# Sending rows to their expert's region of DRAM during the middle block, in a Macaron layer of MoE, Mamba-2 and MoE

## The reference

```python
x = L0_attn_x
x = x + 0.5 * _L0_ffn_ref(_layernorm(x, axis=-1), L0_ffn_router_w, L0_ffn_w1, L0_ffn_w2)
x = x + _L0_attn_ref(_layernorm(x, axis=-1), L0_attn_W_in, L0_attn_conv_w, L0_attn_conv_b, L0_attn_dt_bias, L0_attn_A_log, L0_attn_D, L0_attn_norm_weight, L0_attn_W_out)
x = x + 0.5 * _L0_ffn_ref(_layernorm(x, axis=-1), L0_ffn_router_w, L0_ffn_w1, L0_ffn_w2)
```

```python
logits = jnp.einsum('btd,ed->bte', x, router_w)
top_vals, top_idx = jax.lax.top_k(logits, K)
top_w = jax.nn.softmax(top_vals, axis=-1)
h = jnp.einsum('nd,edh->enh', xf, w1)
h = jnp.square(jax.nn.relu(h))
y = jnp.einsum('enh,ehd->end', h, w2)
```

## Time and profile before

| | us |
|---|---|
| median of three runs | 1234.97 (1228.63 to 1237.66) |
| the profiled execution, its own time | 1231.04 |
| span in its profile | 1229.3 |
| busy PE, DVE, ACT, POOL | 1000.4, 856.4, 663.3, 597.1 |
| granted PE clock, mean | 0.924 |
| first FFN, middle block, second FFN start at | 3.8, 353.1, 900.8 |

### The profile page before, as it was taken

How to read it: one execution, slowest core, us unless ns; L and a number is a source line. 1 busy time by engine, 2 the same in 40 slices (tenths; PEclk the granted TensorE clock), 3 DMA queues, 4 the chain that set the end, 5 groups by cost and what they waited for, 6 DMA issues and landing times. The chain is left out here.

```text
span 1229.3 us, 22312 instructions
## 1 busy us (share of the span) xinstructions
PE 1000.4 (81%) x6980; PEld 868.6 (71%) x7012; DVE 856.4 (70%) x1764; ACT 663.3 (54%) x1624; POOL 597.1 (49%) x608
## 2 busy tenths in 40 slices
PE   4936999999936788888988898989826999999950
PEld 4835999999824556666766666656515999999950
DVE  5586777777638778787778777775366777777647
ACT  1334777777514465656465646565313777777630
POOL 6503666667321446464545453647502466666510
PEclk9998999999966799999899989999757999999985
DMA  8404555555422111111111100000002555655449
GB/s 256 155 1 161 177 172 191 172 173 172 134 83 65 39 40 44 43 44 44 44 44 44 43 27 12 25 18 27 18 13 89 178 201 196 189 190 187 163 139 324
DMA packets 91409, 133.23 MB, mean 108 GB/s; under 512 B 11672, under 2 KB 61344, under 8 KB 91296
## 3 DMA queue, kind: packets, MB, share of 16 engines
q1 hardware_dynamic: 69024, 85.65, 20.8%
q0 software_dynamic: 13824, 37.77, 10.5%
q10 hardware_dynamic: 8448, 8.39, 2.0%
HBM read 96.12 MB, written 35.65 MB: 107 GB/s over the span
## 5 line engine op out<-in xcount | busy, mean ns | idle before, releaser
L463 POOL DMA_INDIRECT ys_d<-xs,row_of x144 | 145.3, 1009 | 158.5 <-ACT xs L551 130.5
L458 POOL DMA_INDIRECT xs<-xn_d,token_of x144 | 146.3, 1016 | 129.9 <-DVE token_of L858 86.6
L876 DVE TENSOR_TENSOR h<-h,pH 128x512 f32<-128x512 f32 (+1 forms) x80 | 50.8, 635 | 120.9 <-ACT h L533 120.6
L1684 DVE SCALAR_TENSOR_TENSOR acc<-bank,cwh,acc 128x511 f32<-128x511 f32 (+2 forms) x120 | 89.6, 747 | 40.8 <-ACT acc L1298 38.0
L871 DVE TENSOR_TENSOR w1l<-raw,w1h 128x512 fp32r<-128x512 f32 x160 | 109.7, 686 | 3.3 <-ACT w1h L528 0.5
L528 ACT ACTIVATE w1h<-raw 128x512 fp32r<-128x512 f32 x160 | 99.5, 623 | 0.6 <-DMA raw<-in_L_ffn_w_dram 0.6
L680 PE MATMUL pY<-w2h,h2h 128*128 x576 | 98.3, 292 | 1.0 <-DVE h2l L881 1.0
L1202 POOL TENSOR_TENSOR yv<-yv,sz 128x512 f32<-128x512 f32 x32 | 40.7, 1272 | 117.3 <-DVE yv L1723 114.1
L881 DVE TENSOR_TENSOR h2l<-h,h2h 128x512 fp32r<-128x512 f32 (+1 forms) x160 | 94.5, 630 | 0.3 <-ACT h2h L538 0.3
L680 PE MATMUL pY<-w2l,h2h 128*128 x576 | 91.4, 280 | 0.0
L680 PE MATMUL pY<-w2h,h2l 128*128 x576 | 91.3, 280 | 0.0
(11 more groups left out here) (269 smaller groups left out, 2953.0 us busy)
## 6 DMA issues: line engine op xcount, KB each, us to landing
raw<-in_L_ffn_w_dram SPq DMA_DIRECT2D x80, 512.0 KB, 3.9
m_yg<-ys_d SPq DMA_DIRECT2D x64, 128.0 KB, 2.2
xs<-ys_d SPq DMA_DIRECT2D x12, 512.0 KB, 6.3
wst<-in_L_ffn_w_dram ACTq DMA_DIRECT2D x8, 512.0 KB, 4.8
xs<-in_L_attn_x_dram SPq DMA_DIRECT2D x8, 512.0 KB, 5.8
xn_d<-xs SPq DMA_DIRECT2D x8, 512.0 KB, 3.9
xr<-in_L_attn_x_dram SPq DMA_DIRECT2D x32, 128.0 KB, 2.3
x_d<-xo SPq DMA_DIRECT2D x32, 128.0 KB, 2.1
```

Of the source, the lines that this page charges most:

```text
L458: pool.indirect_dma_start(out=xg[:, t % NX, :], out_offset=None, in_=xn_d, in_offset=bass.IndirectOffsetOnAxis(ap=token_of[:, t:t + 1], ax ...
L463: pool.indirect_dma_start(out=ys_d, out_offset=bass.IndirectOffsetOnAxis(ap=row_of[:, t:t + 1], axis=0), in_=y[:, t % NX, :], in_offset=No ...
L876: dve.tensor_tensor(h, h, up_bank(q, v), ALU.mult).then_inc(h2_made.sem, 1)
L1684: ins = dve.scalar_tensor_tensor(a, bank[:, 0:GT - n], cwh[:, b, HALO - n:HALO - n + 1], a, ALU.mult, ALU.add)
```

## The change

The second FFN no longer sorts. While the middle block runs, DVE picks each tile's two experts as soon as a group's scores are there (groups of `ROUTE` tiles: seven of four, one of three, one of one). PE counts, with a triangular matmul, how many earlier rows went to each expert, which gives each row its place in its expert's region of a DRAM buffer `bk_d` (8 regions of 4096 + 128 rows). POOL sends each tile there with two indirect DMAs (`send`), one for each choice. A row is 258 floats: 256 values, the row's number and its first choice. `xn2` gets 12 buffers. SP's stores to `xn_d` go.

In the second FFN the counts alone are needed: `plan_units` works out each unit's expert (`expert_i`) and first row (`row_i`). SP writes 128 zero rows behind the end of each region and a block of dead rows, waits for these nine, and then loads each unit as one plain block (`load_unit`, six buffers). The inversion, `token_of` and the gathers are gone there. Where a result goes is worked out from the two extra columns of its rows (`find_rows`). POOL's six tables at the start become others of like size and a zero block of 16 x 258 floats. The first FFN keeps its code, moved into `sort_rows` and `invert`. The middle block has one slot more.

The diff, cut to its core:

```diff
+            def load_unit(q):
+                if q == NP:
+                    sp.wait_ge(experts_known, 2)
+                n = len(tiles_of(q))
+                if q >= RU:
+                    for t in tiles_of(q - RU):
+                        sp.wait_ge(scattered[t % NX].sem, scattered[t % NX].done(t // NX))
+                at = sp.value_load(row_i[0:1, q:q + 1], min_val=0, max_val=DEAD + (E - 1) * P)
+                sp.dma_start(xu[:, q % RU, 0:n, :], bk_d[bass.ds(at, n * P), :].rearrange("(n p) d -> p n d", p=P)).then_inc(units_loaded[q % RU].sem, 16)
+            if not first:
+                load_w1(0)
+                load_w1(1)
+                sp.wait_ge(zeros_made, 1)
+                for e in range(E):
+                    at = sp.value_load(end_i[0:1, e:e + 1], min_val=0, max_val=E * CAP - P)
+                    sp.dma_start(bk_d[bass.ds(at, P), :], zeros[:, e, :]).then_inc(padded, 16)
+                sp.dma_start(bk_d[DEAD:DEAD + E * P, :].rearrange("(n p) d -> p n d", p=P), zeros[:, E:, :]).then_inc(padded, 16)
+                sp.wait_ge(padded, 16 * (E + 1))
+                for q in range(RU):
+                    load_unit(q)
             for q in range(NU):
-                load_w1(q)
+                if not first and q >= RU:
+                    load_unit(q)
+                if first or q >= 2:
...
+                q = unit_of(t)
+                rows = row_of[:, t:t + 1] if first else rowt[:, q % RU, t - tiles_of(q)[0]:t - tiles_of(q)[0] + 1]
+                if not first:
+                    pool.wait_ge(rows_known.sem, rows_known.done(q))
...
+                pe.matmul(pR[0][:, 0:E], c["ones_bf"][:, :], run[:, :], start=True, stop=True).then_inc(counts_out, 1)
...
+            def plan_units():
...
+                counts = pR[0][:, 0:E]
+                link(dve.tensor_scalar(smalli[:, 0, :], counts, float(P - 1), None, ALU.add))
...
+                link(dve.scalar_tensor_tensor(found[:, 0, 0:E], small[:, 6, :], -2.0 * P, cap_e[:, :], ALU.mult, ALU.add))
+                link(dve.tensor_tensor(delta[:, 0, :], found[:, 0, 1:], found[:, 0, 0:E], ALU.subtract))
+                link(dve.tensor_tensor(iota_j[:, 0:NH, :], iota_j[:, 0:NH, :], upto(pairs_to, NH), ALU.is_ge))
+                link(dve.tensor_tensor(picked[:, 0:NH, :], iota_j[:, 0:NH, :], upto(delta[:, 0, :], NH), ALU.mult))
+                link(dve.tensor_reduce(q2[:, 0, 0:NH], iota_j[:, 0:NH, :], AX.X, ALU.add))
+                link(dve.tensor_reduce(q2[:, 1, 0:NH], picked[:, 0:NH, :], AX.X, ALU.add))
+                link(dve.tensor_tensor(q2[:, 1, 0:NH], q2[:, 1, 0:NH], jrow[:, :], ALU.add))
+                link(dve.tensor_scalar(exf[:, 0:NP], q2[:, 0, 0:NP], float(E - 1), None, ALU.min))
+                link(dve.tensor_scalar(expert_i[:, 0:NP], exf[:, 0:NP], float(KD * P), None, ALU.mult))
+                link(dve.tensor_tensor(end_i[:, :], counts, cap_e[:, :], ALU.add))
+                dve.tensor_tensor(row_i[:, 0:NP], q2[:, 1, 0:NP], dead[:, 0:NP], ALU.min).then_inc(experts_known, 1)
...
+            def find_rows(q):
+                n = len(tiles_of(q))
+                number, expert = (xu[:, q % RU, 0:n, D + a:D + a + 1].rearrange("p n a -> p (n a)") for a in range(2))
+                link(dve.tensor_scalar(rowf[:, 0:n], expert, exf[:, q:q + 1], -float(TOK), ALU.is_equal, ALU.mult))
+                dve.tensor_tensor(rowt[:, q % RU, 0:n], rowf[:, 0:n], number, ALU.add).then_inc(rows_known.sem, 1)
...
+ROUTE = (4, 4, 4, 4, 4, 4, 4, 3, 1)
...
-        SLOTS = range(-LEAD, T + 3)
+        SLOTS = range(-LEAD, T + 4)
+        for g, (i0, n) in enumerate(zip(starts, ROUTE)):
+            a = i0 + n + 3
+            b = min(a + 1, T + 2) if i0 + n <= T - 8 else a
+            r = b + 1 if i0 + n <= T - 4 else a
+            PICK_FIRST.setdefault(a, []).append(g)
+            PICK_SECOND.setdefault(b, []).append(g)
+            RANK.setdefault(r, []).append(g)
+            for m in range(n):
+                SEND.setdefault(r + (m if i0 + n <= T - 8 else m // 2 if i0 + n <= T - 4 else 0), []).append(i0 + m)
...
-                if live(s - 2):
-                    sp.wait_ge(norm2_done.sem, norm2_done.done(s - 2))
-                    sp.dma_start(xn_d[(s - 2) * P:(s - 1) * P, :], xn2[:, (s - 2) % 2, :]).then_inc(n_stored[(s - 2) % 2].sem, 16)
...
+            def send(i):
+                g = group_of(i)
+                pool.wait_ge(slots_known.sem, slots_known.done(g))
+                for k in range(TOP):
+                    at = g * GC + i - starts[g]
+                    pool.indirect_dma_start(out=bk_d, out_offset=bass.IndirectOffsetOnAxis(ap=slots[:, k, at:at + 1], axis=0),
+                                            in_=xn2[:, i % RN, :], in_offset=None).then_inc(row_sent[i % RN].sem, 16)
...
+                for i in SEND.get(s, ()):
+                    send(i)
+            for u in range(RN):
+                pool.wait_ge(row_sent[u].sem, row_sent[u].done((T - 1 - u) // RN))
...
-                act.wait_ge(n_stored[i % 2].sem, n_stored[i % 2].done(i // 2 - 1))
-                act.activation(xn2[:, i % 2, :], xo[:, i % 2, :], ACT.Identity, bias=nmr[:, q, 1:2], scale=rstd[:, q, 1:2]).then_inc(norm2_done.sem, 1)
+                if i >= RN:
+                    act.wait_ge(row_sent[i % RN].sem, row_sent[i % RN].done(i // RN - 1))
+                act.activation(xn2[:, i % RN, 0:D], xo[:, i % 2, :], ACT.Identity, bias=nmr[:, q, 1:2], scale=rstd[:, q, 1:2]).then_inc(norm2_done.sem, 1)
...
+            def rank_rows(g, s):
+                n = ROUTE[g]
+                pe.wait_ge(picked.sem, picked.done(g))
+                pe.wait_ge(rank_read.sem, rank_read.done(g - 1))
+                pe.wait_ge(bt_done.sem, bt_done.done(min(s, T - 1)))
+                out = pRank[:, 0:n * E].rearrange("p (a e) -> p a e", e=E)
+                def spread(ap, m):
+                    return ap.rearrange("p (a e) -> p a e", a=1).to_broadcast([P, m, E])
+                pe.matmul(out, c["strict_tri"][:, :], r_both[:, 0:n, :], start=True, stop=False, skip_group_check=True)
+                for m in range(1, n):
+                    pe.matmul(out[:, m:n, :], c["ones_bf"][:, :], spread(r_both[:, m - 1, :], n - m), start=False, stop=False, skip_group_check=True)
+                pe.matmul(out, c["ones_bf"][:, :], spread(run[:, :], n), start=False, stop=True, skip_group_check=True).then_inc(rank_ready.sem, 1)
...
+                for g in RANK.get(s, ()):
+                    rank_rows(g, s)
...
+            def pick_largest(scores, largest, number, onehot, n):
+                routed(dve.tensor_reduce(largest, scores, AX.X, ALU.max))
+                routed(dve.tensor_tensor(r_a[:, 0:n, :], scores, wide(largest, n), ALU.not_equal))
+                routed(dve.scalar_tensor_tensor(r_a[:, 0:n, :], r_a[:, 0:n, :], float(E), r_e[:, 0:n, :], ALU.mult, ALU.add))
+                routed(dve.tensor_reduce(number, r_a[:, 0:n, :], AX.X, ALU.min))
+                routed(dve.tensor_tensor(onehot, r_e[:, 0:n, :], wide(number, n), ALU.is_equal))
+            def pick_first(g):
+                i0, n = starts[g], ROUTE[g]
+                if g == 0:
+                    dve.wait_ge(r_iota, 1)
+                dve.wait_ge(logit_copied.sem, logit_copied.done(i0 + n - 1))
+                at = slice(i0 % RN, i0 % RN + n)
+                number, first = (xn2[:, at, D + a:D + a + 1].rearrange("p n a -> p (n a)") for a in range(2))
+                routed(dve.tensor_scalar(number, r_num[:, 0:n], float(i0 * P), None, ALU.add))
+                pick_largest(logits[:, i0:i0 + n, :], best[:, 0, i0:i0 + n], first, r_oh[:, 0, 0:n, :], n)
+            def pick_second(g):
+                i0, n = starts[g], ROUTE[g]
+                routed(dve.scalar_tensor_tensor(r_b[:, 0:n, :], r_oh[:, 0, 0:n, :], -BIG, logits[:, i0:i0 + n, :], ALU.mult, ALU.add))
+                pick_largest(r_b[:, 0:n, :], best[:, 1, i0:i0 + n], r_second[:, 0:n], r_oh[:, 1, 0:n, :], n)
+                dve.tensor_tensor(r_both[:, 0:n, :], r_oh[:, 0, 0:n, :], r_oh[:, 1, 0:n, :], ALU.add).then_inc(picked.sem, 1)
+            def read_rank(g):
+                n = ROUTE[g]
+                dve.wait_ge(rank_ready.sem, rank_ready.done(g))
+                dve.tensor_tensor(r_slot[:, 0:n, :], pRank[:, 0:n * E].rearrange("p (a e) -> p a e", e=E), r_base[:, 0:n, :], ALU.add).then_inc(rank_read.sem, 1)
+            def find_slots(g):
+                n = ROUTE[g]
+                dve.wait_ge(rank_read.sem, rank_read.done(g))
+                routed(dve.tensor_reduce(r_sum[:, :], r_both[:, 0:n, :].rearrange("p n e -> p e n"), AX.X, ALU.add))
+                routed(dve.tensor_tensor(run[:, :], run[:, :], r_sum[:, :], ALU.add))
+                for k in range(TOP):
+                    routed(dve.tensor_tensor(r_of[:, k, 0:n, :], r_oh[:, k, 0:n, :], r_slot[:, 0:n, :], ALU.mult))
+                for k in range(TOP):
```

(52 more changed lines are left out.)

372 lines of the change are left out of this document (243 added, 129 removed).

## The result

Four runs of the changed kernel have their median at 1267.47 us (1266.49 to 1269.66), against 1232.18 for four of the kernel before: ratio 1.0285, interval 1.0238 to 1.0332. The change makes the kernel 2.9 % slower. The forecast was 1249. Ratios leave out executions more than 1.5 % above the shortest of their kernel. The profiled execution took 1267.51, its span is 1265.8 (before 1229.3).

The account below looks back on a forecast made before the run. It took the second FFN's serial start (45.4 us) as what the change can shorten, its units being PE-bound. End +25.4, start -20.6 and middle +12 gave +16.8 on 1231.0, 1247.8, named 1249; 8-in-10 range 1231 to 1270.

Parts of the forecast that it names:

- Rival 3: Middle slots: sends hold DVE, one operation for 0.95 at each of two sends, half paid, +22; time 1270, chance 0.14.
- Part 1: Start of the second FFN: first transpose at B+24.8 instead of B+45.4 (B: POOL's first operation), -20.6, bounds -17 to -24.
- L1653's row: Profile row: 0.96 us for 32 elements, weighed as evidence that small DVE operations beside POOL's tensor operations are held up.
- Part 2: End of the middle block: 18 late sends, then a 3.81 us drain, move the FFN's start by +25.4, bounds +20 to +32.
- Part 3: Middle slots: sends on POOL cost 8, picks and ranks 4, together +12, between 3 and 25.
- my list: The seven middle slots expected to be hit by the sends: 15, 19, 23 and 27 to 30.
- The ranks ahead of the output product: Slot 32: PE ranks tiles 24 to 27 before the output product, making it and POOL's power 1.65 later.
- Rival 2: Middle block: PE's granted clock stays at full in slow slots, so the kernel gets faster; time 1226, chance 0.06.
- Part "units at PE 100 %: 0": Second FFN's running units: PE is already fully busy and gathers hidden, so removing them gives 0.
- a sign of being wrong: Listed trace evidence against the forecast; here, DVE operations of 1 us beside sends.
- Rival 4: Start of the second FFN: pads or unit loads take long, gain 10 instead of 20.6; time 1259, chance 0.08.
- Rival 1: Middle block absorbs nearly all added work, 0 to 3 of the 12; time 1239, no measurable change, chance 0.22.

Follow-up runs that it names:

- picks alone: Changed kernel without the sends of tiles 0 to 22, the 18 at the end kept, units reading dead rows: 1251.05 us, 1.0109 of before.
- again: The changed kernel profiled and timed once more with no edit: median 1265.44 us of five, 1.0247 of before.
- first edit: Changed kernel with the zero rows filled by ScalarE in place of GpSimd's memset: 1258.23 us in one execution, start 27.71.
- second edit of the start: Changed kernel with the 1032 KB block of dead rows stored first, before the wait for the experts: 1264.71 us in one execution, start 26.84.
- both edits of the start: Changed kernel with zero rows filled by ScalarE and the dead block stored first: 1257.32 us, 1.0191 of before, start 24.11.
- late sends: Changed kernel, zeros by ScalarE, dead block first, the 18 last sends moved behind the FFN's first nine scatters, units reading dead rows: 1238.84 us, 1.0017 of before.
- split pads: Changed kernel, zeros by ScalarE, dead block first, four of the eight pad stores on ScalarE's queue: 1256.2 us, 1.0181 of before, start 23.68.
- neither picks nor sends: Changed kernel without picks, ranks and all sends, units reading dead rows: 1221.6 us, 0.988 of before; repeated, 1227.24.
- sends alone: Changed kernel with all 64 sends to constant rows, no picks or ranks, counts set to 1024, units reading dead rows: 1253.47 us, 1.0154 of before.

## Why the prediction was right or wrong

The direction, the places and most mechanisms were right; the size was not: +14 was forecast against the median, +35 measured. Over all executions on record it is less, +31: a mean of 1265.8 for 9 of the changed kernel, 1234.8 for 33 of the kernel before. 1267 lies inside the stated range, but at the end that Rival 3 held, for a reason that the runs do not bear out. Two steps failed: the zero block called hidden (Part 1), and the clock, which the sum had at nothing. Three terms were too small: the ninth store, the end of the queue, the units.

**Part 1, the start of the FFN, failed as a step.** "POOL fills the zero block ... meanwhile ... hidden" is refuted. With POOL's fill beside it DVE's L953 took 3.04 us longer than with ScalarE's (3.21 for 0.17), and with it the whole plan: experts are known at B+9.8, where I had B+6.8. I had read L1653's row as something that the picks might suffer, and not looked at the one long POOL operation of my own part 1. The Trainium skill (SBUF — State Buffer, Who interferes with whom) says that a `tensor_scalar` can run in a two-port mode, and that of it and GpSimd whoever comes first has the shared ports for its whole instruction; the trace agrees, 3.21 us beside GpSimd's fill and 0.17 beside ScalarE's. The second error is the ninth store: I gave all nine 2.4, though this one has eight times the bytes. It landed after 5.7. From the first pad's issue to the ninth store's are 8.1 us (961.99 to 970.06) where I had 8.8, which gave 0.7 back; 3.0 + 3.3 - 0.7 are 5.6, and 0.2 less in small steps makes the 5.4 missing. Sum: -15.2 for -20.6, at the wrong side of the bound of -17. With both causes removed the start is 24.1, against my 24.8.

**Part 2, the end, was right in its 18 sends, 1.265 us each, and short in two terms.** I put the drain 2.4 us behind the start of the last send. It starts 3.3 behind it (939.70, 943.0), 0.9 more. And it took 5.28 and not 3.81, 1.5 more. Those are the 2.4 missing. With picks alone, so 18 sends and none before them, the end is 27.88: 4.1 of the 32.0 come with the 46 sends of the middle slots. The drain's rows, kernel after, the middle block and the two FFN blocks (shortest, median and longest of two):

```profile
L1143 POOLq DRAIN  x1: 5280/5280/5280, 943.0 to 943.0; - x1
...
L194 POOLq DRAIN  x2: 3810/4871/5932, 348.2 to 1226.1; - x2
```

**Part 3, the middle slots, was right in its sum at full clock, in part by luck:** +12.4 in slots 5 to 30 for 12. The split was 8 for the sends and 4 for picks and ranks; measured in slots 20 to 23, 2.2 and 0.8 of 2.6 (each alone adds up to a little more than both). For slot 23 the sends were given 1.65 and cost 1.7. The luck is in the others: slot 11, not in my list, and slots 15 and 19, given 0.85 and 0.9, cost 2.9 to 3.0 each, 1.3 of it the picks as in slot 23, while slots 28 to 30, given 3.0 together, come to less than 0.6. Slots 11, 15, 19, 23 and 27 are hit by 2.4 to 3.0, slots 28 and 29 by 1.0 and 1.2, and slot 30, which I counted among the hit, gains 1.7. Slots 10, 14, 18, 22 and 26 gain 0.6 to 1.4, which pays the picks back; in slot 22 it is the cover that I had named, DVE's wait for tanh. POOL's wait for PE before the state's decay, which I took as the cover, fell from 33.0 us to 5.6 in the same window. The ranks ahead of the output product, 1.65 in my sum, are rather 0.5 to 1.1: from the start of slot 31 to the last power are 20.3 and 20.0 us before (at clocks of 0.59 and 0.66), 21.4 and 20.5 after (0.60 and 0.67). Two of the variants take 23.3 there, at 0.50.

**What I left out is the clock.** Rival 2 let it fall out to one side, the better. In the profiled execution it went to the other: of the middle block's 22.6 us, 12.4 are the slots at full clock, 1.1 lies behind the start of slot 31 (21.4 to the last power for 20.3), and the remaining 9 are what the falls of the clock cost more than before. The blocks of the seven executions with the changed middle block, in the order after, again, first edit, second, both, late sends, split pads: 564.4, 551.9, 556.2, 564.7, 560.7, 564.7, 559.5, mean 560.3; before 541.8 and 545.0, mean 543.4. That is +16.9, so 4 over the instructions' 13 on average. Whether the change itself brings the additional falls isn't settled. The two profiles with neither picks nor sends had 558.9 and 549.3, as long as some with both, with instructions that at full clock take no longer than before. But both lie above the average of their kernel. Taking off each mean time what the profiles have outside the block (678 us there, 690 before, 704 after), the block is some 545 in the kernel before, 544 to 546 with neither and 562 with both: an estimate, good to some 3 us, and by it the 4 come with the picks and sends.

**Part "units at PE 100 %: 0"** was off by 3. The first FFN's units come every 6.14 us (before 6.15), the second's every 6.18 or 6.19 instead of 6.13. Timeline of two transposes of the kernel after:

```profile
1059.58 0.60 PE L737 MATMUL pT<-ident,xu 128*128 128x128 f32 x4
1065.77 0.60 PE L737 MATMUL pT<-ident,xu 128*128 128x128 f32 x4
```

About 30 such units give 1.6; the first two units give 0.7, and what lies behind the start of the last unit 1.1. The 0.05 a unit is there with dead rows too; its cause was not tried.

Taken together, what the forecast lacked in the profiled execution is some 9 of clock, 5.4 at the start, 3.5 in the units and behind them, and 2.4 at the end. Rival 3 named nearly the right time, 1270, by luck: beside sends alone DVE's small operations keep their length, and the few long ones of 1.4 to 2.9 us, which I had listed as a sign of being wrong, last as long as POOL's tensor operations behind the send. They are six, not two a slot. Rival 4 (the start gains only 10) had the right kind of reason; it gained 15. Rival 1 is excluded by the slots.

## What to carry to other kernels

Work moved out of a serial prologue is only hidden if its last inputs are ready well before the block ends: here 9 of 32 tiles were late, and their sends with the drain made the end 26 us longer, more than the whole prologue's gain of 15. Count what is left over when the loop ends, not what fits inside it. A prologue that is a chain of VectorE's small operations had a long fill on GpSimd not beside it but in it, 3 us of it, and the store that all unit loads waited for was to be priced by its bytes (5.7 us for 1032 KB, 2.2 for 129) and issued first. An operation held on its own engine doesn't show as a wait for the other: look at its length as well as at the waits. And when TensorE's granted clock falls in some slots and not in others from one execution to the next, compare slots at full clock before a block's length is charged to the change.

## What the runs showed that was not expected

The drain of POOL's queue at the end of a block grew with the indirect DMAs that the block issued, but for the blocks with 144. Without any it took 0.96, with 18 1.52, with 46 4.12, with 64 5.28, with 72 5.93 and with 90 7.40: from 64 on 0.082 us for each. Rows of the kernels with picks alone (18) and with late sends (the first FFN with 144, the second with 90):

```profile
L1144 POOLq DRAIN  x1: 1523/1523/1523, 934.8 to 934.8; - x1
```

```profile
L194 POOLq DRAIN  x2: 3810/5606/7402, 348.9 to 1204.0; - x2
```

It isn't proportional throughout: the 144 gathers and scatters of the first FFN take 3.81 in every kernel. Why, no run here shows. My prediction took the 3.81 of 144 for a constant.

The falls of the clock follow a pattern that comes back to the hundredth: the changed kernel and two of its variants (dead block first, and late sends) have slots 4 and 17 at 0.69 with 22.2 and 22.1 us, in three separate executions. In two other executions of the same middle block both are at full clock (the second one, and both edits of the start). Slot 4, in which no kernel has a pick or a send, has only three lengths in the fourteen profiles, within 0.03 us: 16.56, 19.14 and 22.24, at 1.00, 0.82 and 0.69. The kernel before has the first in one profile and the second in the other; with neither picks nor sends it is the second and the third. What decides between them, no run here shows. Slots 4 and 17 of the kernel with the second edit of the start:

```profile
477.89:500.12 22.23, 20.59 (x83) 15.08 (x83) 13.23 (x30) 9.18 (x31) 8.12 (x8) 0.69 0.09 25
690.18:712.24 22.06, 20.39 (x86) 15.16 (x86) 13.42 (x32) 10.38 (x33) 7.83 (x8) 0.69 0.10 31
```
